# One layernorm pass for two nested ones, and query, key and value projections as three products of rounded float32 parts, in a Perceiver block on one core

## The chip, the cores and the metric

One core of a Trainium2 chip runs the whole program in one launch. The metric is the device time of that launch in microseconds (us), from runs of the same program; lower is better. Engines are named PE (TensorE, matrix products), ACT (ScalarE), DVE (VectorE), POOL (GpSimd) and SP (SyncE, which issues the DMAs).

## The reference, cut to what matters

A Perceiver block on 256 tokens of width 512: cross-attention to 4096 context rows, self-attention with 16 heads, and a feed-forward part (FFN) with quantised weights. What the change touches is the self-attention's entry:

```python
def _layernorm(x, axis=-1, eps=1e-05):
    m = jnp.mean(x, axis=axis, keepdims=True)
    v = jnp.var(x, axis=axis, keepdims=True)
    return (x - m) / jnp.sqrt(v + eps)
...
def _L0_attn_ref(X, ln_w, ln_b, W_in, W_out):
    mu = jnp.mean(X, axis=-1, keepdims=True)
    var = jnp.mean(jnp.square(X - mu), axis=-1, keepdims=True)
    Xn = (X - mu) * jax.lax.rsqrt(var + LN_EPS) * ln_w + ln_b
    qkv = jnp.einsum('bsd,df->bsf', Xn, W_in)
    Q, K, V = jnp.split(qkv, 3, axis=-1)
    ...
    return out + X
...
x = x + _L0_xattn_ref(_layernorm(x), ctx_512, ...)
x = x + _L0_attn_ref(_layernorm(x), ln_w, ln_b, W_in, W_out)
x = x + _L0_ffn_ref(_layernorm(x), w1, w2, w3)
```

So x is normalised to h1 (which is also added back as the residual), h1 is normalised again, scaled and shifted to Xn, and Xn goes through the projection to queries, keys and values. Everything is float32. In the FFN each weight matrix is divided by its mean magnitude, rounded and clipped to -1, 0 or 1.

## The kernel before, in words

Five instruction streams are written out by hand, one for each engine; semaphores alone tie them together, so the order within each stream is the order of the code. Tokens are handled as two tiles of 128. The cross-attention fills the first 450 us or so. It ends with the output products (L615 to L617): for each head and tile three products of rounded float32 parts (type f32r), high by high, high by low and low by high. ACT makes the high part of the output weights by a copy into f32r (L1002) and DVE the low part by a subtraction (L1212).

Then comes the stretch around the change.

DVE, for each tile t: the residual sum out of PSUM (L1346), a layernorm to h1 and a second one of h1 to z1. A layernorm is batch statistics (L1170), aggregation (L1174), an addition of epsilon (L1178), a wait for ACT's square root (L940), a reciprocal (L1182), one refining step on numbers of one column (L1185 to L1190), and the normalisation of 128x512 (L1194). Behind them DVE has, in this order: the rotation of the tile-0 key block (rotate, L1360 to L1366), the total of the magnitudes of w1 (weight_total, L1375), the rotation of the tile-0 query block, the copy of the tile-0 values (L1371), the mean and scale of w1 (L1380, L1383), the rotation of the key block of tile 1, the total of w3, the rotation of the query block, the scale of w3, the copies of the transposed keys (L1388), and then the softmax maxima (L1407), among which stand the clips of the rounded weights (L1427): w1 behind the fifth maximum, w3 behind the sixth.

PE: the transposes of z1 of tile 0 (L578) into bank 0, then `project(t, j)` (L767), four float32 products of 128x512 for tile t and j = 0, 1, 2 (key, query and value weights): (0,0), (0,1), the transposes of tile 1, (0,2), the weight sum of w1 (weight_sum, L758, which needs DVE's total), (1,0), (1,1), the weight sum of w3, the transposes of the rotated blocks with one half of (1,2) between them, the other half, and the attention scores (L809).

ACT: roots (L940); the scaling and shift of the transposed tile into hTn (scale_shift, L1054, four operations of 128x128 a tile); the absolute sums of w1, w3 and w2 (abs_sum, L1064), four for each; the copies of the projected blocks out of PSUM (natural_copy, L1070); the copies of the transposed queries (L1075). Its order is: roots, scale_shift(0), roots and two sums, natural_copy(0,0), two sums, natural_copy(0,1), scale_shift(1), three sums, natural_copy(1,0), two sums, natural_copy(1,1), and so on.

POOL: h1 is added to x_sb (L542), once for each tile, when the output products are done; then, as soon as DVE has the scale of w1 (L1383), w1 and w3 are scaled (L549) and rounded (L556) in eight pieces each; w2 follows when DVE has clipped w3.

SP: the loads of the projection weights wink_sb, winq_sb and winv_sb (L467 to L469) and of w1 (L470) when the last attention product is done, and those of w3, w2 and the output weights (L472 to L474) when the output products are done.

Of the kernel before, what the change touches and what calls it, by code (L numbers as in the profile page):

```python
# [6 lines left out]
TT = TOK // 128  # L7
DM = 512
DK = DM // 128
# [14 lines left out]
EPS = 1e-5  # L24
# [3 lines left out]
def program(nc, x_in, ctxT, kcos, ksin, qcos, qsin, wq, wkcq, wqr, wkr, wkv, wo,  # L28
# [24 lines left out]
    with ctx:  # L53
# [50 lines left out]
        v_sb = at("v_sb", C + 16 * KB, [128, TT, DM])  # L104
# [42 lines left out]
        acc = small("acc", [128, 2, 2, 128])  # L147
        cT = small("cT", [128, FG, TOK])
# [9 lines left out]
        eps = small("eps", [128, 1])  # L158
        rs = small("rs", [128, TT])
# [66 lines left out]
        hTn_done = sem("hTn_done")  # L226
        hTq_done = [sem(f"hTq_done{k}") for k in range(2)]
# [53 lines left out]
        win_in = sem("win_in")  # L281
# [88 lines left out]
        def _(sp):  # L370
# [96 lines left out]
            sp.dma_start(wink_sb[:, :, :], w_k).then_inc(win_in, 16)  # L467
            sp.dma_start(winq_sb[:, :, :], w_q).then_inc(win_in, 16)
            sp.dma_start(winv_sb[:, :, :], w_v).then_inc(win_in, 16)  # L469
# [12 lines left out]
        def _(pool):  # L482
# [57 lines left out]
            for t in range(TT):  # L540
                pool.wait_ge(z_done, TT + 2 * t + 1)
                nc.gpsimd.tensor_tensor(x_sb[:, t, :], x_sb[:, t, :], h1[:, t, :], ALU.add).then_inc(x2_done, 1)  # L542
# [32 lines left out]
        def _(pe):  # L575
# [184 lines left out]
            def project(t, j, chunks=range(DK)):  # L760

                w = (wink_sb, winq_sb, winv_sb)[j]
                pe.wait_ge(win_in, 48)
                for c in chunks:
                    if j == 0:
                        pe.wait_ge(hTn_done, t * DK + c + 1)
                    last = nc.tensor.matmul(bank(QKV_BANK[t][j]), hTn[:, c, t * 128:(t + 1) * 128], w[:, c, :],  # L767
                                            start=(c == 0), stop=(c == DK - 1))
                if c == DK - 1:
                    last.then_inc(qkv_done, 1)  # L770

            pe.wait_ge(z_done, TT + 2)
            tile_transposes(z1[:, 0, :], 0, zT_done)
            project(0, 0)
            pe.wait_ge(x1_done, TT)
            project(0, 1)
            pe.wait_ge(z_done, TT + 4)
            tile_transposes(z1[:, 1, :], 1, zT_done)
            project(0, 2)
            weight_sum(0, bank(7, 0, 1))  # L780
            project(1, 0)
            project(1, 1)
            pe.wait_ge(wmean_done, 1)
            weight_sum(1, bank(7, 0, 1))
            for t in range(TT):
                for j in range(2):
                    pe.wait_ge(rot_done, 2 * t + j + 1)
                    if t == 1 and j == 1:
                        pe.wait_ge(qT_done, 1)
                    tile_transposes(qkn[:, t, j, :], 2 if j == 1 else t, qkT_done)  # L790
                if t == 0:
                    pe.wait_ge(v_copied, 1)
                    project(1, 2, range(DK // 2))
            project(1, 2, range(DK // 2, DK))
# [142 lines left out]
        def _(act):  # L937
# [111 lines left out]
            def scale_shift(t):  # L1049
# [3 lines left out]
                for c in range(DK):  # L1053
                    nc.scalar.activation(hTn[:, c, t * 128:(t + 1) * 128], bank(t, c * 128, (c + 1) * 128), ACT.Identity,  # L1054
                                         bias=lnp[:, 1, c:c + 1], scale=lnp[:, 0, c:c + 1]).then_inc(hTn_done, 1)

# [21 lines left out]
            root(3, slice(0, 1))  # L1078
            root(4, slice(0, 1))
            scale_shift(0)  # L1080
            root(5, slice(1, 2))
            abs_sum(0, 0)
            root(6, slice(1, 2))
# [49 lines left out]
            root(7, slice(0, 1))  # L1133
# [3 lines left out]
            root(8, slice(1, 2))  # L1137
# [16 lines left out]
        def _(dve):  # L1154
# [185 lines left out]
            for h in range(len(SPLIT_STEPS), XH):  # L1340
                if h == 10:
                    context_low(XH // 2 - 1)
                output_weight_low(h)
            for t in range(TT):
# [3 lines left out]
                layernorm(x_sb, h1, t, t + 1)  # L1348
                dve.wait_ge(z_done, TT + 2 * t + 1)
                layernorm(h1, z1, t, t + 1)  # L1350
# [40 lines left out]
            rotate(0, 0)  # L1391
            weight_total(0)
# [64 lines left out]
            for t in range(TT):  # L1457
                dve.wait_ge(ao_done, t + 1)
                layernorm(x_sb, h2, t, t + 1, bank(6 + t), x3_done)
                dve.wait_ge(z_done, 3 * TT + t + 1)  # L1460
# [110 lines left out]
```

## Time and profile before

| what | value |
|---|---|
| median of 3 runs | 564.32 us (563.91 to 564.53) |
| span of the profiled execution | 564.2 us |
| busy: PE / DVE / ACT / POOL | 94% / 83% / 65% / 28% of the span |
| mean granted clock of PE | 0.991 of full |
| DMA | 107.41 MB, mean 190 GB/s |

The profiled execution is one run of its own; its time is its span, from the first to the last instruction, and it lies between the fastest and the median of the runs above. Times on the axis below are us from the start of the span. A "releaser" is what ended an engine's idle time. A float32 product of 128x512 shows as two records, a rounded one as one; products overlap, so a group's time is shorter than the sum of its records.

### The profile page before, as it was taken

Reading aid. Unit: us, or ns where it says so; the run is one execution under the profiler, and the core shown is the slowest. Engines: PE = TensorE matmul, PEld = TensorE weight load, DVE = VectorE, ACT = ScalarE, POOL = GpSimd, SP = SyncE. Lnnn points to the kernel's source line nnn. Section 1 sums busy time; section 2 is a strip of 40 time slices with the busy share of each in tenths; the row PEclk is TensorE's granted clock in tenths of the full one; section 3 lists DMA queues with packets and bytes.
Section 4 is the critical chain, followed back from the end, with each engine's and each line's share of the span. In section 5 each row is a group of like instructions: output and inputs, shape, how many; then the busy total and the mean of one; then the engine's idle time right before and its main releaser. Section 6 shows DMA issues by size and latency. Waiting matters only on the chain.

```text
span 564.2 us, 10021 instructions
## 1 busy us (share of the span) xinstructions
PE 528.2 (94%) x3799; PEld 353.0 (63%) x3803; DVE 468.4 (83%) x708; ACT 366.0 (65%) x447; POOL 159.0 (28%) x202
## 2 busy tenths in 40 slices
PE   7899976799999999999999999999997998999996
PEld 3767643366666666666667666766676784455443
DVE  3566997999989999999999999999996447478686
ACT  2125433888788688688688787787786444886441
POOL 2378965101202202202202202202000001496501
PEclk9989999999999999999999999999998998999999
DMA  8979468399999999999999999999999997500001
GB/s 314 345 259 288 156 116 220 87 200 196 198 195 200 202 197 203 208 209 212 203 204 195 203 204 194 198 210 195 204 198 178 226 416 305 238 1 1 1 0 38
DMA packets 287806, 107.41 MB, mean 190 GB/s; under 512 B 276896, under 2 KB 277920, under 8 KB 286368
## 3 DMA queue, kind: packets, MB, share of 16 engines
q1 hardware_dynamic: 287776, 107.01, 87.6%
q8 instruction: 18, 0.29, 0.2%
q14 instruction: 12, 0.10, 0.0%
HBM read 37.26 MB, written 0.52 MB: 67 GB/s over the span
## 4 chain that ended last, share of the span: by engine, by line
PE 57%; DVE 17%; POOL 8%; DMA 6%; issue 6%; ACT 4%; SPq 0%; ACTq 0%; DVEq 0%; POOLq 0%
PE ps L665 15%; PE ps L667 8%; PE ps L647 7%; PE ps L649 7%; PE ps L648 7%; DMA pT<-split 6%; POOL qrope L498 5%; DVE rows L1273 4%; DVE split L1255 3%; PE ps L767 3%; POOL keys L509 2%; POOL stage L510 1%; PE ps L876 1%; PE ps L615 1%; PE ps L617 1%
## 5 line engine op out<-in xcount | busy, mean ns | idle before, releaser
L665 PE MATMUL ps<-pT,VH 128*128 128x256 f16 x1024 | 196.6, 274 | 2.1 <-DMA pT<-split 2.0
L667 PE MATMUL ps<-pT,VL 128*128 128x128 f16 x1024 | 183.3, 220 | 0.0
L1273 DVE TENSOR_SCALAR_CACHE_REDUCE rows<-ps,qback 128x1024 f32<-128x1024 f32 x128 | 163.5, 1280 | 16.0 <-PE ps L649 15.9
L1033 ACT ACTIVATE split<-rows,rz 128x2048 f16<-128x2048 f32 x64 | 124.7, 1994 | 67.8 <-DVE rz L1221 67.7
L1255 DVE SCALAR_TENSOR_TENSOR split<-rows,rz,split 128x2048 f16<-128x2048 f32 x64 | 150.3, 2350 | 1.3 <-issue 1.2
L1019 ACT ACTIVATE rows<-rows,negm 128x2048 f32<-128x2048 f32 x64 | 127.2, 1987 | 0.2 <-DVE negm L1278 0.2
L665 PEld LDWEIGHTS ps<-pT,VH 128*128 128x128 f16 x1024 | 100.5, 98 | 42.6 <-DMA pT<-split 4.8
L667 PEld LDWEIGHTS ps<-pT,VL 128*128 128x128 f16 x1024 | 100.6, 98 | 27.5
L528 POOL TENSOR_TENSOR ctx_c<-acc 128x128 f32<-128x128 f32 x32 | 24.7, 772 | 296.8 <-ACT acc L1008 296.8
L647 PE MATMUL ps<-KH,qcur 128*128 128x512 f16 x256 | 97.1, 379 | 3.3 <-DVE rows L1273 3.3
L649 PE MATMUL ps<-KH,qcur 128*128 128x512 f16 x256 | 97.0, 379 | 0.0
L648 PE MATMUL ps<-KL,qcur 128*128 128x512 f16 x256 | 97.0, 379 | 0.0
L498 POOL TENSOR_TENSOR qrope<-qrope,qrot 128x384 f32<-128x384 f32 x32 | 38.2, 1214 | 22.6 <-DVE qrot L1311 22.4
L649 PEld LDWEIGHTS ps<-KH,qcur 128*128 128x128 f16 x256 | 25.0, 98 | 30.2
L696 PE MATMUL ps<-hTq,wq_sb 128*128 128x256 f32 x128 | 30.4, 392 | 1.5 <-ACT hTq L946 0.8
L647 PEld LDWEIGHTS ps<-KH,qcur 128*128 128x128 f16 x256 | 25.1, 98 | 10.2 <-DVE rows L1273 4.3
L1305 DVE TENSOR_TENSOR qrope<-ps,qcos_sb 128x768 f32<-128x768 f32 x16 | 15.2, 950 | 19.0 <-PE ps L707 18.9
L696 PEld LDWEIGHTS ps<-hTq,wq_sb 128*128 128x128 f32 x128 | 24.4, 195 | 7.5 <-issue 3.3
L648 PEld LDWEIGHTS ps<-KL,qcur 128*128 128x128 f16 x256 | 25.0, 98 | 2.3
L707 PE MATMUL ps<-qhk,wkcq_sb 128*128 128x256 f32 x96 | 23.7, 386 | 2.6 <-DVE qrot L1311 2.6
L549 POOL TENSOR_SCALAR w_sb<-w_sb,wscale 128x704 f32<-128x704 f32 x24 | 20.5, 872 | 14.1 <-DVE wscale L1383 9.9
L707 PEld LDWEIGHTS ps<-qhk,wkcq_sb 128*128 128x128 f32 x96 | 17.6, 190 | 7.1 <-issue 5.0
(175 smaller groups left out, 638.3 us busy)
## 6 DMA issues: line engine op xcount, KB each, us to landing
w_sb<-w SPq DMA_DIRECT2D x3, 2816.0 KB, 15.6
wq_sb<-wq SPq DMA_DIRECT2D x4, 1024.0 KB, 7.3
wo_sb<-wo SPq DMA_DIRECT2D x16, 256.0 KB, 4.2
wkcq_sb<-wkcq SPq DMA_DIRECT2D x4, 768.0 KB, 10.3
keys<-ctxT SPq DMA_DIRECT2D x8, 256.0 KB, 7.1
stage<-ctxT SPq DMA_DIRECT2D x16, 128.0 KB, 9.0
stage<-kcos SPq DMA_DIRECT2D x8, 256.0 KB, 9.0
stage<-ksin SPq DMA_DIRECT2D x8, 256.0 KB, 9.5
```

The lines of the kernel that those rows point to most:

```text
L498: nc.gpsimd.tensor_tensor(qrope[:, h % 4, part], qrope[:, h % 4, part], qrot[:, h % 2, part], ALU.add).then_inc(qrope_done, 1)
L647: nc.tensor.matmul(o, q[0], KH[:, key], start=True, stop=False)
L648: nc.tensor.matmul(o, q[0], KL[:, key], start=False, stop=False)
L649: last = nc.tensor.matmul(o, q[1], KH[:, key], start=False, stop=True)
L665: nc.tensor.matmul(bank(6 + r % 2, 0, 256), VH[:, 4 * b + k, :], p.rearrange("p x q -> p (x q)"), start=(b == 0 and k == 0), stop=False)
L667: last = nc.tensor.matmul(bank(6 + r % 2, 0, 128), VL[:, 4 * b + k, :], p[:, 0, :], start=False, stop=(b == 7 and k == 3))
L696: last = nc.tensor.matmul(bank(0, a * TOK, (a + 1) * TOK), wq_pair(wq_sb, q)[:, c, head], hTq[:, c, :], start=(c == 0), stop=(c == DK - 1))
L707: last = nc.tensor.matmul(ps[:, o:o + TOK], wkcq_sb[:, h // WQG % 2, h % WQG, c * 128:(c + 1) * 128], qhk[:, h, :], start=True, stop=True)
L1019: nc.scalar.activation(part, part, ACT.Exp, bias=negm[:, k:k + 1], accum_out=zpart[:, k, half:half + 1]).then_inc(exp_done, 1)
L1033: nc.scalar.activation(split[:, split_slot(r, half), :, 0, :], rows[:, k, half * 2048:(half + 1) * 2048].rearrange("p (b k) -> p b k", k=1 ...
L1255: nc.vector.scalar_tensor_tensor(out=split[:, split_slot(r, half), :, 1, :], in0=rows[:, k, half * 2048:(half + 1) * 2048].rearrange("p (b ...
L1273: nc.vector.tensor_scalar(rows[:, k, c * 1024:(c + 1) * 1024], ps[:, score_bank(s) * 512:(score_bank(s) + 2) * 512], qback[:, r // 2:r // ...
```

## The change

One pass of statistics serves both layernorms: DVE computes mean and variance v of x once and from them v + eps and v(1 + eps) + eps². ACT takes the roots of both in one operation, and DVE writes z1 (the twice normalised tile) first and h1 second, both directly from x. The second pass of statistics and its root are gone. POOL's residual add now waits for h1 by a semaphore of its own.

The projections use rounded float32 parts. ACT copies each of the three weight matrices into f32r (128x2048, one operation), DVE subtracts to get the low parts in place. ACT's scale_shift writes each tile twice: four operations into f32r (hTn_hi), then the four into hTn; DVE subtracts the one from the other (hTn_lo). PE then does high by high, high by low, and low by high, 12 products of 128x512 for each (t, j) in place of 4 float32 ones. Buffers move (v_sb, the new parts), and the three weight loads get a semaphore each.

```diff
-            sp.dma_start(wink_sb[:, :, :], w_k).then_inc(win_in, 16)
+            sp.dma_start(wink_sb[:, :, :], w_k).then_inc(win_in[0], 16)
...
             for t in range(TT):
-                pool.wait_ge(z_done, TT + 2 * t + 1)
+                pool.wait_ge(h1_done, t + 1)
...
+            def project_hi(t, j, chunks=range(DK)):
+                hi, lo = ((wink_hi, wink_lo), (winq_hi, winq_lo), (winv_hi, winv_lo))[j]
+                pe.wait_ge(win_hi_done, j + 1)
+                pe.wait_ge(win_lo_done, j + 1)
                 for c in chunks:
...
+                    pe.wait_ge(hTn_hi_done, t * DK + c + 1)
+                    for w in (hi, lo):
+                        nc.tensor.matmul(bank(QKV_BANK[t][j]), hTn_hi[:, t, c, :], w[:, c, :],
+                                         start=(c == 0 and w is hi), stop=False)
+            def project_lo(t, j):
+                pe.wait_ge(hTn_lo_done, t + 1)
+                for c in range(DK):
+                    last = nc.tensor.matmul(bank(QKV_BANK[t][j]), hTn_lo[t][:, c, :],
+                                            (wink_hi, winq_hi, winv_hi)[j][:, c, :], start=False, stop=(c == DK - 1))
+                last.then_inc(qkv_done, 1)
-            pe.wait_ge(z_done, TT + 2)
+            pe.wait_ge(z1_done, 1)
             tile_transposes(z1[:, 0, :], 0, zT_done)
-            project(0, 0)
+            project_hi(0, 0)
             pe.wait_ge(x1_done, TT)
-            project(0, 1)
-            pe.wait_ge(z_done, TT + 4)
+            project_hi(0, 1)
+            pe.wait_ge(z1_done, 2)
             tile_transposes(z1[:, 1, :], 1, zT_done)
-            project(0, 2)
+            project_lo(0, 0)
+            project_lo(0, 1)
+            project_hi(0, 2)
+            project_lo(0, 2)
             weight_sum(0, bank(7, 0, 1))
-            project(1, 0)
-            project(1, 1)
+            project_hi(1, 0)
+            project_lo(1, 0)
+            project_hi(1, 1)
+            project_lo(1, 1)
...
-                    project(1, 2, range(DK // 2))
-            project(1, 2, range(DK // 2, DK))
+                    project_hi(1, 2, range(DK // 2))
+            project_hi(1, 2, range(DK // 2, DK))
+            project_lo(1, 2)
...
                 for c in range(DK):
+                    nc.scalar.activation(hTn_hi[:, t, c, :], bank(t, c * 128, (c + 1) * 128), ACT.Identity,
+                                         bias=lnp[:, 1, c:c + 1], scale=lnp[:, 0, c:c + 1]).then_inc(hTn_hi_done, 1)
+                for c in range(DK):
...
+            def both_roots(t):
+                act.wait_ge(ve2_done, 2 * t + 2)
+                nc.scalar.activation(sd2[:, t, :], ve2[:, t, :], ACT.Sqrt).then_inc(sd_done, 1)
...
-            root(3, slice(0, 1))
-            root(4, slice(0, 1))
+            qkv_weight_high(0)
+            qkv_weight_high(1)
+            both_roots(0)
+            qkv_weight_high(2)
             scale_shift(0)
-            root(5, slice(1, 2))
+            both_roots(1)
             abs_sum(0, 0)
-            root(6, slice(1, 2))
             abs_sum(0, 1)
             natural_copy(0, 0)
...
+            qkv_weight_low(0)
+            qkv_weight_low(1)
             for t in range(TT):
                 dve.wait_ge(xo_done, t + 1)
                 nc.vector.tensor_tensor(x_sb[:, t, :], bank(2 + t), x_sb[:, t, :], ALU.add).then_inc(x1_done, 1)
                 dve.wait_ge(x1_done, t + 1)
-                layernorm(x_sb, h1, t, t + 1)
-                dve.wait_ge(z_done, TT + 2 * t + 1)
-                layernorm(h1, z1, t, t + 1)
+                two_layernorms(t)
+            normalised_low(0)
+            qkv_weight_low(2)
...
             rotate(0, 0)
+            normalised_low(1)
             weight_total(0)
             rotate(0, 1)
             value_copies(0)
```

The new functions of DVE, of which two_layernorms is statistics and aggregation as before, the two sums (ve2), the wait for the root, five operations on two columns, and the two normalisations:

```python
def qkv_weight_low(j):
    dve.wait_ge(win_hi_done, j + 1)
    nc.vector.tensor_tensor((wink_lo, winq_lo, winv_lo)[j][:, :, :].rearrange("p c d -> p (c d)"),
    ...
                            ALU.subtract).then_inc(win_lo_done, 1)
def normalised_low(t):
    dve.wait_ge(hTn_done, DK * (t + 1))
    nc.vector.tensor_tensor(hTn_lo[t][:, :, :], hTn[:, :, t * 128:(t + 1) * 128], hTn_hi[:, t].bitcast(f32),
                            ALU.subtract).then_inc(hTn_lo_done, 1)
def two_layernorms(t):
    ...
    nc.vector.tensor_scalar(z1[:, t, :], x_sb[:, t, :], mv[:, t, 0:1], rs2[:, t, 1:2],
                            ALU.subtract, ALU.mult).then_inc(z1_done, 1)
    nc.vector.tensor_scalar(h1[:, t, :], x_sb[:, t, :], mv[:, t, 0:1], rs2[:, t, 0:1],
                            ALU.subtract, ALU.mult).then_inc(h1_done, 1)
```

## Rows read from the trace of the kernel before

**Rows 1.** Page, part 1: busy us, share of the span, instructions.
```profile
PE 528.2 (94%) x3799; PEld 353.0 (63%) x3803; DVE 468.4 (83%) x708; ACT 366.0 (65%) x447; POOL 159.0 (28%) x202
```

**Rows 2.** Timeline of PE: start, us, line, tiles, count, idle before, releaser.
```profile
455.17 0.40 PE L616 MATMUL ps<-wo_lo,ctxl_hi 128*128 128x512 f32 x1
...
469.73 0.39 PE L617 MATMUL ps<-wo_hi,ctxl_lo 128*128 128x512 f32 x1
...
473.11 5.37 PE L767 MATMUL ps<-wink_sb,hTn 128*128 128x512 f32 x8 [0.64 <-ACT hTn L1054]
...
489.27 3.60 PE L767 MATMUL ps<-winq_sb,hTn 128*128 128x512 f32 x8
```

**Rows 3.** Timeline of DVE, the same columns.
```profile
464.71 0.69 DVE L1346 TENSOR_TENSOR x_sb<-ps,x_sb 128x512 f32<-128x512 f32 x1 [4.64 <-PE ps L617]
...
467.62 0.55 DVE L1194 TENSOR_SCALAR h<-x_sb,mv,rs 128x512 f32<-128x512 f32 x1
...
470.38 1.38 DVE L1194 TENSOR_SCALAR z<-h,mv,rs 128x512 f32<-128x512 f32 x1
...
486.61 0.16 DVE L1383 RECIPROCAL wscale<-wmean 128x1 f32<-128x1 f32 x1
...
511.97 2.46 DVE L1427 TENSOR_SCALAR w1b<-w1b 128x5632 bf16<-128x5632 bf16 x1
...
515.48 1.61 DVE L1427 TENSOR_SCALAR w3b<-w3b 128x5632 bf16<-128x5632 bf16 x1
```

**Rows 4.** Chain of waits, 425 to 565 us: start, us, engine, tile, line.
```profile
471.81 0.67 PE ps L578 x4
...
512.06 2.38 DVE w1b L1427
```

**Rows 5.** Stretches of 1 us: length, busy engines, PE clock, DMA, GB/s.
```profile
474.00:475.00 1.00, 1.00 (x2) 0.33 (x1) 0.61 (x4) 1.00 (x3) 0.00 (x0) 0.50 0.94 406
```

**Rows 6.** Timeline of ACT.
```profile
466.39 0.29 ACT L940 ACTIVATE sd<-mv,eps 128x1 f32<-128x1 f32 x1 [6.22 <-DVE mv L1174]
...
472.50 1.50 ACT L1054 ACTIVATE hTn<-ps,lnp 128x128 f32<-128x128 f32 x4 [3.06 <-PE ps L578]
...
478.51 0.60 ACT L1070 ACTIVATE qkn<-ps 128x512 f32<-128x512 f32 x1 [0.20 <-PE ps L767]
...
482.44 1.50 ACT L1054 ACTIVATE hTn<-ps,lnp 128x128 f32<-128x128 f32 x4
...
489.47 0.60 ACT L1070 ACTIVATE qkn<-ps 128x512 f32<-128x512 f32 x1 [1.18 <-PE ps L767]
...
492.91 0.60 ACT L1070 ACTIVATE qkn<-ps 128x512 f32<-128x512 f32 x1
```

**Rows 7.** Timeline of POOL.
```profile
475.75 1.26 POOL L542 TENSOR_TENSOR x_sb<-x_sb,h 128x512 f32<-128x512 f32 x1 [4.29 <-DVE h L1194]
486.87 7.17 POOL L549 TENSOR_SCALAR w_sb<-w_sb,wscale 128x704 f32<-128x704 f32 x8 [9.85 <-DVE wscale L1383]
...
506.98 5.97 POOL L556 TENSOR_SCALAR w3b<-w_sb 128x704 bf16<-128x704 f32 x8
```

**Rows 8.** By line and shape, 425 to 565 us: busy, mean ns, idle.
```profile
L1212 DVE TENSOR_TENSOR wo_lo<-wo_sb,wo_hi 128x512 fp32r<-128x512 f32 x16 | 10.3, 693 | 7.8 <-ACT wo_hi L1002 7.7
...
L1033 ACT ACTIVATE split<-rows,rz 128x2048 f16<-128x2048 f32 x2 | 4.0, 1995 | 0.1
```

**Rows 9.** Timeline of SP's DMA issues.
```profile
451.16 0.68 SPq L468 DMA_DIRECT2D winq_sb<-w_q  x1
```

**Rows 10.** DMA issues of 450 to 452.3 us: KB each, us to landing.
```profile
winq_sb<-w_q SPq DMA_DIRECT2D x1, 1024.0 KB, 9.3
```

**Rows 11.** What writes rot_tmp: count, duration ns least, median, most.
```profile
L1360 DVE TENSOR_TENSOR rot_tmp<-qkn,acs x4: 424/424/781, 479.1 to 493.5; 128x256 f32<-128x256 f32 x4
```

**Rows 12.** Timeline of PE, 106 to 118 us.
```profile
113.23 0.39 PE L647 MATMUL ps<-KH,qcur 128*128 128x512 f16 x1 [2.00 <-DVE rows L1273]
```

**Rows 13.** The same columns as rows 5, in a longer stretch.
```profile
80.00:120.00 40.00, 29.67 (x169) 14.50 (x168) 35.15 (x60) 24.62 (x36) 12.39 (x15) 1.00 0.76 165
```

## What the change should do to the time, worked out before it ran

> **What bounds the kernel now.** I read the page first: TensorE (PE) is busy 94% of the 564.2 us span [rows 1]. That is an average. The change touches only what follows the cross-attention, some 458 us on, so I read that stretch: first the chain of waits, then the timelines of PE, ScalarE (ACT), VectorE (DVE) and GpSimd (POOL), then the durations by line. The reader is to see four things.
>
> First, PE ends the output products at 470.12 (469.73 + 0.39 [rows 2]) and then stands, because z of the first tile is ready only at 471.76 (470.38 + 1.38 [rows 3]); the chain goes on with the transposes at 471.81 [rows 4]. Second, the six projections are full float32 and their PE time is the chain from there: the first takes 5.37 us, the fifth 3.60 [rows 2], because PE's granted clock was 0.50 in between, the lower of its two levels (1.2 of 2.4 GHz) [rows 5]. Third, ACT's queue holds, in one order, the copies that PE and DVE wait for and the absolute sums of the FFN weights; from the copy of the first query/key block at 478.51 to the last at 492.91 it stood still only 1.18 us [rows 6]. Fourth, the clip of w1 on DVE is on the chain [rows 4] and took 2.46 us, the equal clip of w3 1.61 [rows 3]: the first ran beside POOL's rounding of w3, which ended at 512.95 (506.98 + 5.97 [rows 7]); the clip ended 1.48 after that, nearly its whole length alone.
>
> **The change, part by part.** Times are on the axis of the profiled run; its span of 564.2 us stands 0.1 below the median of 564.32.
>
> *Splitting the weights.* Three rounded copies on ACT: 128x2048 takes 1.99 us [rows 8]. Three subtractions on DVE: 128x512 takes 0.69 [rows 8], so four times the length is at most 2.8, and about 2.2 if the fixed part is paid once. ACT and DVE are free from about 459 and 460; the query weights land at 460.5 (451.16 + 9.3 [rows 9, 10]). So the copies end at 461 and 463, the two subtractions ahead of the layernorm at 463.2 and 465.4. The first residual sum then starts about 0.7 after its 464.71 [rows 3]. I cost all this at nothing: PE's output products cover it until 470.12. Without that cover the 0.7 would count. The third copy and subtraction come later, below.
>
> *One set of statistics.* Before, the first layernorm of tile 0 ended at 468.17 (467.62 + 0.55 [rows 3]) and a second one followed. Now the normalised z comes at the end of the first, with about three small operations more (0.2 each): 468.17 + 0.6 + 0.7 = 469.4. That is before PE is free, so the transposes start at 470.1, 1.7 us earlier. What is late next is the ACT copy out of PSUM.
>
> *ACT writes each tile twice.* Eight scalings in place of four, which took 1.50 [rows 6]: 470.6 to 473.4. PE starts on the first chunk at about 471.2 and needs 16 rounded products for the first two high parts. 64 intervals between 455.17 and 469.73 [rows 2] give 0.2275 us each, so 3.6 us, to 474.8. The root for tile 1 is queued behind the eight scalings: 473.4. From root to end of the normalisation took 1.78 (466.39 [rows 6] to 468.17), now 1.9: z of tile 1 at 475.2, its transposes at 475.9.
>
> *The low part of tile 0.* PE next wants the low products, and these wait for a DVE subtraction (128x512, 0.69 alone) queued behind both outputs of tile 1: it starts at 475.8, just when POOL starts its residual add, 1.26 us long [rows 7]. Beside POOL, z took 1.38 where the same operation takes 0.55 alone [rows 3], and an operation with two SBUF inputs 0.78 for 0.42 [rows 11]. Bounds: not slowed, done at 476.5; held off wholly, 477.7. I take 477.1, by the two-input row, the nearest. The Trainium skill, "GPSIMD Engine Reference", section Key points, says that POOL shares its SBUF interfaces with VectorE and contends with instructions that have two SBUF inputs; by it the 476.5 drops out. It does not say which side waits; the rows do, DVE. Four low products (0.9) follow, so ACT's first copy comes at 478.2 against 478.51: all the earlier start is back to 0.3.
>
> *ACT's line from there.* 14.40 us before (478.51 to 492.91), less 1.18 idle, plus four more scalings of tile 1 (1.4): 14.6. The last copy stands at 492.8 against 492.91.
>
> *A new wait on PE.* The weight sum sits in PE's order between the tiles and needs a total from DVE. DVE's total is now queued behind the low part of tile 1, which needs ACT's eighth scaling of tile 1. Before, those scalings began 3.93 after the first copy (482.44 [rows 6]); now they begin at 482.1, eight last 2.9, so 485.0. Subtraction to 485.7, total to 485.9. PE, done with tile 0 at 482.2, stands about 3.8 us. Then the key projection of tile 1 takes 12 x 0.2275 = 2.7, to 488.8; ACT comes to its copy at 489.4, so this wait is hidden if the clock stays up.
>
> *The projections themselves.* Three rounded products take 0.68 against 0.86 for a float32 one (3.60 for four, overlaps left out [rows 2]), so PE does some 4.3 us less work in all. It is off the path: ACT and DVE set the pace now. On the path is the second half of the last projection, 8 x 0.2275 = 1.82 against 1.72: +0.1. So the scores start within 0.1 of before; call this shift d = 0, with bounds -0.7 (low part not slowed) and +1.2 (clock, below).
>
> *POOL.* Its 26.1 us of weight rounding (486.87 to 512.95 [rows 7]) starts on the weight scale, which DVE computed at 486.61 [rows 3]. Now DVE has, after the total at 485.9, a rotation (four operations, 1.3 by the 0.42 [rows 11]), a value copy (0.7) and two small ones: 488.2. POOL starts 1.6 later and ends at 514.5. The clip of w1 waits at its old place, 512.0 + d, and if POOL holds it off as before it ends at 514.5 + 1.48 = 516.0 against 514.43. The DVE operations behind it are on the chain, so **+1.55 us** reaches the end. A d below 1.5 is swallowed by it. SP issues the same loads in the same order, with one semaphore each in place of a common one, which I cost at nothing.
>
> Sum: 564.2 + 1.5, plus 0.1 to the median: 565.7 us.
>
> **The rivals.**
>
> *A, the clip is not held longer than before.* If DVE gets in between POOL's instructions, only d is left: 564.3 to 565.4. For: there were only two POOL instructions left beside the clip before. Against: it finished 1.48 after POOL, so it had got almost nothing done beside it.
>
> *B, the low part of tile 0 is held off wholly, or PE's clock falls before it.* Then ACT's line and POOL's start move 0.6 to 1.0 further, and the end with them: 566.3 to 567.2. For the hold: z beside the same POOL add. PE would stand about 0.6 and 1.2 us around the transposes; before, stands of 1.7 and 0.64 [rows 2] were followed by the lower clock [rows 5], but one of 2.00 was not [rows 12, 13].
>
> *C, the clock falls in the 3.8 us stand.* A fall after less standing is in the trace [rows 2, 5], so I hold it likely. The price is bounded by the first projection of before, 5.37 against 3.60: up to 1.7 us on PE, 0.5 of it hidden, so d = 1.2: under the 1.55, no change of the forecast; with A, 565.4. The Trainium skill, "TensorE: Matmul & The Clock Gate", Part 1, says the throttled state is the default and activity releases it; by it the fall is all but certain.
>
> *D, faster.* The subtraction of tile 0 is not slowed by POOL (done by 476.5) and the clip is not held: ACT's line is 0.7 earlier, rotations of tile 1 have more of POOL's late start free of contention (up to 0.8, half of the 1.6 by which it is later), and the clip may run at its 1.61 (-0.85), so 562.0 to 563.6. The point that decides is whether the first query/key copy comes before 477.6. Against: both rows of contention.
>
> *E, the change does not do what it says:* no sign; the weights are split on the chip and three products stand in the code.
>
> **How the numbers follow.** Forecast 0.51 (565.2 to 566.2, by 0.5 either way on POOL's end, which is also the likeliest case's own range), A with or without C 0.20, B 0.13, D 0.16. The forecast's point is 565.7. Leaving out the lower three quarters of D and the top of B gives 563.2 to 567.0. A measurement tells this kernel from no change at about 0.2%, 1.13 us: faster means below 563.2, slower above 565.45. Faster: three quarters of D, 0.12. Slower: three quarters of the forecast's band lie above 565.45, 0.38, with nearly all of B: 0.5. The rest, 0.38, is the same.
>
> **What would show it.** Transposes at about 470.1; first copy on ACT at 478.2; PE standing some 3.8 us ahead of the weight sum, released by DVE's total at 485.9; POOL starting at 488.4 and ending at 514.5; the clip of w1 at 3.5 us or more. Wrong would be: a first copy before 477.6, a last one after 494, a POOL start before 487.5, or a clip that ends before POOL does.

## The result, and the profile after

| | before | after |
|---|---|---|
| median of 22 runs of each, same chips | 564.64 us (560.98 to 566.95) | 566.93 us (565.39 to 572.37) |
| ratio of the runs, 95% interval | | 1.0046 (1.0029 to 1.0064) |
| profiled execution: span, mean granted clock of PE | 564.2 us, 0.991 | 570.5 us, 0.982 |
| end of the output products, on its own axis | 470.12 us | 475.25 us |
| **tail**: from there to the end of the span | 94.08 us | 95.25 us |

The change costs half a per cent: +2.3 us between the medians, where +1.4 was forecast.

Two things have to be settled before the two profiles are compared. First, a run's time is about 1.8 us more than its span (after: 572.37 against 570.5; the runs below give 1.75 to 1.91). So the profiled run of before, with its span of 564.2, took about 566.0 us: it stands above all three runs of the table ahead of the prediction, and not between them as is said there. The profiled run of after is the slowest of its 22. Second, the spans differ by 6.3 us, but 5.1 of that has built up by the end of the output products, which come 5.13 us later. In that run PE's granted clock was low in two stretches more than in before's, 11 to 15 and 96 to 100 us, and this row is from the first of them (stretches of PE: length, busy us, PE clock, DMA share, GB/s):

```profile
13.00:14.00 1.00, 1.00 (x4) 0.50 1.02 395
```

The runs don't put this down to the change: e1 and e2, which split the weights just as after does, have one such stretch each and end the output products at 468.97 and 469.94 us, the four profiles without the change have one to three and end them at 469.22 to 472.35, and after has four. So everything below is read on another axis: "+x" is x us after the end of the last output product, in each kernel's own profile.

The busy shares of the page say nothing of it; PE's is 93% for 94% [rows 1]:

```profile
PE 530.0 (93%) x3823; PEld 360.2 (63%) x3827; DVE 473.8 (83%) x703; ACT 373.7 (65%) x456; POOL 162.2 (28%) x202
```

PE's timeline after (columns as in [rows 2]) shows where the time goes:

```profile
474.86 0.39 PE L636 MATMUL ps<-wo_hi,ctxl_lo 128*128 128x512 f32 x1
475.10 0.60 PE L597 MATMUL ps<-ident,z 128*128 128x128 f32 x4
476.33 0.47 PE L787 MATMUL ps<-wink_hi,hTn_hi 128*128 128x512 f32 x1 [0.64 <-ACT hTn_hi L1086]
...
481.41 1.19 PE L794 MATMUL ps<-wink_hi,hTn_lo 128*128 128x512 f32 x4 [0.40 <-DVE hTn_lo L1403]
...
490.22 0.58 PE L777 MATMUL ps<-wtot,ones 128*128 128x1 f32 x2 [3.56 <-DVE wtot L1461]
490.66 0.78 PE L787 MATMUL ps<-wink_hi,hTn_hi 128*128 128x512 f32 x1
...
494.22 1.88 PE L794 MATMUL ps<-wink_hi,hTn_lo 128*128 128x512 f32 x4
...
497.78 1.07 PE L794 MATMUL ps<-winq_hi,hTn_lo 128*128 128x512 f32 x4
```

The transposes follow the products without the 1.69 us that PE stood before. Then PE stands 3.56 us for DVE's total, a wait that before did not have (its weight sum followed the products with no idle time), and behind it the key projection of tile 1 runs from 490.66 to 496.10: 5.4 us, where twelve products at the spacing of [rows 2] take 2.7. Its last four take 1.88, those of the query projection right behind 1.07. The stretches give the reason (length, busy us of PE, PE's weight loads, DVE, ACT and POOL, PE clock, DMA share, GB/s):

```profile
491.00:492.00 1.00, 1.00 (x3) 0.80 (x3) 1.00 (x3) 1.00 (x1) 0.00 (x0) 0.50 1.04 442
...
494.00:495.00 1.00, 1.00 (x3) 0.79 (x3) 0.00 (x0) 0.00 (x0) 1.00 (x2) 0.50 0.00 0
```

PE's clock is at its lower level (1.2 of 2.4 GHz), and in the second of these stretches DVE and ACT stand idle: they wait for this projection. DVE's timeline (columns as in [rows 3]):

```profile
480.67 0.69 DVE L1403 TENSOR_TENSOR hTn_lo<-hTn,hTn_hi 128x512 fp32r<-128x512 f32 x1
...
484.33 1.41 DVE L1452 TENSOR_TENSOR qkn<-rot_tmp 128x256 f32<-128x256 f32 x1
489.40 0.69 DVE L1403 TENSOR_TENSOR hTn_lo<-hTn,hTn_hi 128x512 fp32r<-128x512 f32 x1 [3.66 <-ACT hTn L1089]
490.01 0.15 DVE L1461 TENSOR_REDUCE wtot<-wpart 128x1 f32<-128x4 f32 x1
...
492.06 0.16 DVE L1469 RECIPROCAL wscale<-wmean 128x1 f32<-128x1 f32 x1
...
518.99 1.62 DVE L1514 TENSOR_SCALAR w1b<-w1b 128x5632 bf16<-128x5632 bf16 x1
```

ACT's, as in [rows 6]:

```profile
482.64 0.60 ACT L1117 ACTIVATE qkn<-ps 128x512 f32<-128x512 f32 x1 [1.05 <-PE ps L794]
...
496.14 0.60 ACT L1117 ACTIVATE qkn<-ps 128x512 f32<-128x512 f32 x1 [2.41 <-PE ps L794]
...
499.56 0.58 ACT L1117 ACTIVATE qkn<-ps 128x512 f32<-128x512 f32 x1
```

and POOL's, as in [rows 7]:

```profile
475.34 1.27 POOL L561 TENSOR_TENSOR x_sb<-x_sb,h 128x512 f32<-128x512 f32 x1 [18.39 <-PE ps L636]
480.83 4.62 POOL L561 TENSOR_TENSOR x_sb<-x_sb,h 128x512 f32<-128x512 f32 x1 [4.22 <-DVE h L1425]
492.32 6.97 POOL L568 TENSOR_SCALAR w_sb<-w_sb,wscale 128x704 f32<-128x704 f32 x8 [6.87 <-DVE wscale L1469]
...
512.39 5.97 POOL L575 TENSOR_SCALAR w3b<-w_sb 128x704 bf16<-128x704 f32 x8
```

The low part of tile 0 (480.67) is not slowed beside POOL's residual add; the add is, 4.62 us for its usual 1.26 [rows 7], and behind it the last operation of DVE's rotation (484.33) takes 1.41 us, where its like at 490.93 takes 0.42. And the clip of w1 (518.99) begins 0.63 us after POOL's rounding ended (512.39 + 5.97 = 518.36) and takes 1.62, not 2.46 as in [rows 3]. The chain of waits that ended last is now this (columns as in [rows 4]):

```profile
487.98 1.40 ACT hTn L1089 x4
489.44 0.57 issue
490.22 0.58 PE ps L777 x2
490.80 3.62 PE ps L787 x8
494.42 1.69 PE ps L794 x4
496.14 0.60 ACT qkn L1117
...
521.91 1.53 DVE w3b L1514
```

The clip of w1 has left it, the low part of tile 1 and the slow projection have come in.

### The profile page after: what moved, and what is told of

Same layout as the page of the kernel before. It is cut to its first block, busy times and chain, and to the rows that moved or that the text cites. A ratio compares the mean times of both kernels' runs of the same rounds, so it can differ in the third digit from the quotient of the medians.

```text
span 570.5 us, 10076 instructions
## 1 busy us (share of the span) xinstructions
PE 530.0 (93%) x3823; PEld 360.2 (63%) x3827; DVE 473.8 (83%) x703; ACT 373.7 (65%) x456; POOL 162.2 (28%) x202
## 4 chain that ended last, share of the span: by engine, by line
PE 57%; DVE 16%; POOL 8%; issue 7%; DMA 6%; ACT 5%; SPq 0%; ACTq 0%; DVEq 0%; POOLq 0%
PE ps L684 15%; PE ps L686 8%; PE ps L666 7%; PE ps L668 7%; PE ps L667 7%; DMA pT<-split 6%; POOL qrope L517 5%; DVE rows L1321 4%; DVE split L1303 3%; POOL keys L528 2%; PE ps L634 1%; PE ps L636 1%; POOL stage L529 1%; PE ps L635 1%; PE ps L908 1%
## 5 line engine op out<-in xcount | busy, mean ns | idle before, releaser
L715 PE MATMUL ps<-hTq,wq_sb 128*128 128x256 f32 x128 | 31.7, 404 | 1.5 <-ACT hTq L978 0.8
L737 PE MATMUL ps<-qrope,wqr_sb 128*64 128x256 f32 x96 | 13.4, 418 | 8.8 <-POOL qrope L517 7.8
```

Of the source, the lines that this page charges most:

```text
L715: last = nc.tensor.matmul(bank(0, a * TOK, (a + 1) * TOK), wq_pair(wq_sb, q)[:, c, head], hTq[:, c, :], start=(c == 0), stop=(c == DK - 1))
```

## The experiments

All tails, measured as above. The clip column gives start and length of the clip of w1; "low clock" the us after the products in which PE's granted clock was under 1, the last 2 us of a span left out ("end only": nowhere else). Each row is one profiled run. Tail and median time don't agree to better than a us or two: e9 and e10 are below before in the median (0.997 and 0.9976) with tails of 92.39 and 93.30 against e11's 92.48.

| kernel | tail | first / last copy on ACT | POOL start / end of w3 rounding | scores | clip of w1 | low clock |
|---|---|---|---|---|---|---|
| before | 94.08 | 8.39 / 22.79 | 16.75 / 42.83 | 29.02 | 41.85, 2.46 | 3 to 7 |
| e11, before | 92.48 | 8.10 / 21.09 | 15.05 / 41.20 | 27.34 | 40.18, 2.50 | none |
| e12, before | 92.43 | 8.09 / 21.09 | 15.05 / 41.13 | 27.32 | 40.16, 2.45 | none |
| after | 95.25 | 7.39 / 24.31 | 17.07 / 43.11 | 30.90 | 43.74, 1.62 | 13 to 20 |
| e1 order | 92.53 | 7.39 / 21.79 | 13.61 / 40.19 | 28.13 | 40.96, 1.62 | 22 to 25 |
| e2 warm | 95.66 | 7.38 / 21.80 | 17.07 / 43.28 | 27.30 | 40.14, 4.62 | 49 to 56 |
| e3 one layernorm | 90.57 | 4.93 / 19.18 | 13.14 / 39.28 | 25.42 | 38.27, 2.49 | none |
| e4 parts only | 100.18 | 12.07 / 26.49 | 21.77 / 47.97 | 32.00 | 44.85, 4.60 | 11 to 15, 52 to 59 |
| e5 before, warm | 92.35 | 8.09 / 21.09 | 15.05 / 41.12 | 27.32 | 40.15, 2.46 | end only |
| e6 late add | 95.64 | 7.38 / 24.18 | 17.06 / 44.35 | 30.16 | 42.99, 2.83 | 13 to 20 |
| e7 warm, late clips | 97.01 | 7.39 / 21.80 | 17.08 / 43.29 | 27.32 | 46.27, 1.62 | 70 to 77 |
| e8 split on DVE | 95.23 | 7.16 / 19.54 | 12.62 / 39.21 | 25.53 | 44.46, 1.62 | 67 to 74 |
| e9 one layernorm, clips | 92.39 | 4.93 / 19.19 | 13.15 / 39.28 | 25.42 | 41.10, 1.62 | 49 to 52 |
| e10 split on DVE, clips | 93.30 | 7.20 / 19.57 | 12.63 / 39.12 | 26.18 | 41.85, 1.62 | 50 to 54 |

**e1: the low part of tile 1 behind the weight scale.** PE's weight sum of w1 then waits for no subtraction.

```diff
             rotate(0, 0)
-            normalised_low(1)
             weight_total(0)
...
             weight_scale(0, bank(7, 0, 1))
+            normalised_low(1)
```

> Times count from the end of the output products; the tail is from there to the end of the span (94.1 us in the profile before, 95.3 in the one after). Theory 1, PE's stand on the total of w1 and the half clock behind it are the loss: with the low part of tile 1 moved behind the scale of w1 on VectorE, the stand shrinks below 1.3 us, the last query/key copy comes at +22.0 (after: +24.3), the scores at +28.3 (after: +30.9), GpSimd's rounding starts at +13.5 (after: +17.1), and the tail is 92.7, the time 564.3. Rival, ScalarE's extra scalings and the splitting are the loss and the stand is covered: the stand only moves in front of the low products of tile 1, the scores stay at +30.9, the tail at 95.3, the time at 566.9.

Measured: 563.38 us, 0.9984 (0.9952 to 1.0016) of before. PE no longer stands for the total of w1, only 1.15 us for the low part, in the middle of the key projection and without a fall of the clock there. It does stand 2.61 us for the total of w3 later, and there the clock falls (22 to 25 in the table):

```profile
480.21 0.28 PE L777 MATMUL ps<-wtot,ones 128*128 128x1 f32 x2
480.79 0.47 PE L787 MATMUL ps<-wink_hi,hTn_hi 128*128 128x512 f32 x1 [0.30 <-ACT hTn_hi L1086]
...
484.03 1.19 PE L794 MATMUL ps<-wink_hi,hTn_lo 128*128 128x512 f32 x4 [1.15 <-DVE hTn_lo L1403]
...
490.58 0.35 PE L777 MATMUL ps<-wtot,ones 128*128 128x1 f32 x2 [2.61 <-DVE wtot L1461]
```

One moved operation takes the whole loss away: the interval lies below that of after (1.0029 to 1.0064), and the tail is 2.7 us shorter than after's and equal to e11's. The order on DVE is the cause of the loss against before. The move does two things at once, the scores come 2.8 us earlier than in after (28.13) and POOL starts 3.5 us earlier (13.61), and the clip, which starts behind POOL's rounding here too, is not held. e2 does only the first of the two.

**e2: the stand filled.** PE multiplies an identity matrix into a bank that is overwritten, while it waits for the total.

```diff
             project_lo(0, 2)
+            keep_busy(15, 7)
             weight_sum(0, bank(7, 0, 1))
```

> 15 empty products in front of the weight sum fill PE's stand, nothing else is changed. Theory 1, the lower clock behind the stand cost 2.4 us of the projection: it takes 2.7 us in place of 5.1, the last copy comes at +21.9, the scores at +28.4. Then the clip of w1 starts at +41.4, before GpSimd ends its rounding at +43.1: if it is held as in the kernel before, it takes about 3.2 us and the tail is 94.5 (time 566.1); if it is not held it takes 1.6, tail 92.8 (time 564.4). Rival, the clock is no part of it: scores at +30.9, tail 95.3, time 566.9 or more by the fill.

Measured: 567.92 us, 1.0051 (1.002 to 1.0083). The clock stays up and the scores start 3.6 us earlier than after (27.30 against 30.90), yet the tail is 0.4 us longer. DVE's and POOL's timelines show what takes the place of the slow projection:

```profile
510.08 4.62 DVE L1515 TENSOR_SCALAR w1b<-w1b 128x5632 bf16<-128x5632 bf16 x1
```

```profile
507.23 5.99 POOL L575 TENSOR_SCALAR w3b<-w_sb 128x704 bf16<-128x704 f32 x8
```

The clip now meets POOL's rounding and ends at 514.70, 1.48 after the rounding ends at 513.22. The clip is 2.12 us longer than e11's 2.50, and longer than the 3.2 that was expected. Another 1.1 comes behind it on PE:

```profile
518.06 1.12 PE L854 MATMUL ps<-ident,prob 128*128 128x128 f32 x8 [2.24 <-ACT pT L1165]
519.11 1.97 PE L842 MATMUL ps<-kT,qT 32*128 32x256 f32 x8
```

DVE's next maximum is queued behind the held clip, so PE stands 2.24 us, its clock falls, and eight score products take 1.97 in place of 1.13. From the end of the clip to the end of the span it is 50.90 us here and 49.8 to 50.0 in before, e11, after, e1 and e3. e4 has the same: clip of 4.60, a stand of 2.23 us, low clock, 50.73.

**e3: the single layernorm alone,** with the projections in float32 as before (four products, `project` as it was, no parts of weights or of hTn).

```diff
-            project_hi(0, 0)
+            project(0, 0)
...
-            project_lo(0, 0)
-            project_lo(0, 1)
-            project_hi(0, 2)
-            project_lo(0, 2)
+            project(0, 2)
```

> The single pass of statistics alone, projections in float32 as before. Theory 1: the transposes start 1.7 us earlier, PE does not fall to half clock in the first projection (1.8), the first copy comes at +5.1, the last at +19.3, the scores 3.5 us earlier than before, tail 90.6; against the median of before, where not every run has that fall, 561.5. Rival, the layernorm's gain is given back on ScalarE's line as in the kernel after: first copy at +8, tail 94, time 564.6.

Measured: 561.22 us, 0.994 (0.9911 to 0.9969). The first copy on ACT comes 3.17 us earlier than in e11, all else 1.9 earlier, and the clip, held just as before (2.49), ends 1.9 earlier. e1, which differs from it by the parts alone, has a tail 2.0 us longer.

**e4: the parts alone,** with the two layernorms of before.

```diff
-                two_layernorms(t)
+                layernorm(x_sb, h1, t, t + 1)
+                dve.wait_ge(z_done, TT + 2 * t + 1)
+                layernorm(h1, z1, t, t + 1)
```

> The rounded parts alone, with the two layernorms of before. Theory 1: the first transposes come 2.4 us later than in the kernel after and everything behind them with them, tail 97.6, time 569.2. Rival, ScalarE's line or PE's stand hides the layernorm: tail 95.3, time 566.9.

Measured: 571.61 us, 1.0115 (1.0064 to 1.0167), more than either expectation. The tail is 7.7 us longer than e11's. In the order on PE the low products of tile 0 stand behind the transposes of tile 1, and these wait for its second layernorm:

```profile
479.24 0.66 PE L597 MATMUL ps<-ident,z 128*128 128x128 f32 x4 [2.91 <-DVE z L1244]
479.84 1.32 PE L794 MATMUL ps<-wink_hi,hTn_lo 128*128 128x512 f32 x4
```

So the first copy comes at 12.07, and later the clip is held as in e2. Together with the single layernorm the parts cost 2.8 against e11 and not 7.7; the layernorm alone gains 1.9 (e3). The two halves do not add.

**e5: before, with PE kept busy in its stand of 1.69 us** before the transposes.

```diff
+            keep_busy(8, 1)
             pe.wait_ge(z_done, TT + 2)
```

> The kernel before, with 8 empty products in PE's stand ahead of the first transposes. Theory, the half clock in its first projection belongs to some runs and not to the kernel: with the fill the first projection takes 3.6 us in place of 5.4, the last copy comes at +21.0 (before: +22.8), the tail is 92.3 in place of 94.1; the median falls by 1.8 times the share of runs that have the fall, about 0.9, to 563.7. Rival, the fall moves to another place or is no loss: tail 94.1, time 564.6.

Measured: tail 92.35, as expected, but 565.64 us, 1.0006 (0.9982 to 1.003), not lower. If the fall of the clock in [rows 5] were in every run of before, filling the stand would give 1.7 us, a ratio of 0.997; that lies outside, unless the fill itself costs something. A fall in half of the runs would be inside. e11 and e12 point the same way: the fall is in one of three profiles of before.

**e6: POOL's residual add of tile 1 behind the rounding of w1.**

```diff
+            residual_add(0)
...
             weight_round(0, w1_sb, w1b)
+            residual_add(1)
```

> The kernel after, with GpSimd's residual add of tile 1 moved behind the rounding of w1, so that VectorE's subtractions and the first rotation run with GpSimd idle. Theory, VectorE's operations with two inputs are served and GpSimd's add waited (4.62 us for 1.27): the low part of tile 0 stays at 0.69 us, the first copy at +7.4, the last operation of the first rotation takes 0.42 in place of 1.41, the tail stays at 95.3. The prediction's step, GpSimd slows the subtraction: the first copy comes earlier than +7.4.

Measured, a single run: 569.45 us, tail 95.64. The add takes 1.27 there, and the last operation of the first rotation 0.43 in place of 1.41. The first copy, POOL's start and the weight sum do not move (7.38, 17.06, and PE stands 3.60), so the contention around the add is real and delays none of them. The tail says less: the scores come 0.74 us earlier than in after, but the moved add stands in POOL's row of weight work, whose rounding of w3 ends 1.24 us later and holds the clip (2.83).

**e7: e2 with both clips later,** behind the seventh and eighth maximum, clear of POOL.

```diff
-                if v in (2, 3):
-                    clip(v - 2, (w1b, w3b)[v - 2])
+                if v in (4, 5):
+                    clip(v - 4, (w1b, w3b)[v - 4])
```

> The kernel with PE's stand filled, and the clips of w1 and w3 two places later in VectorE's order, behind the seventh and eighth maximum, where GpSimd has ended the rounding of w3. Theory, the clip held by GpSimd's rounding gave back what the clock gained: both clips take 1.6 us, scores at +27.3, tail 92.7 in place of 95.7, time 565.0 in place of 567.9. Rival, the hold is not on the path or the later clips delay the rounding of w2 onto it: tail 95.7, time 567.9.

Measured: 569.41 us, 1.0086 (1.0055 to 1.0117). The clips take 1.62 each, but POOL's scaling and rounding of w2 start only when w3 is clipped, and now DVE waits for that; the tail is longer than both expectations:

```profile
531.16 1.63 DVE L1515 TENSOR_SCALAR w2b<-w2b 128x5632 bf16<-128x5632 bf16 x1 [4.84 <-POOL w2b L575]
```

**e8: hTn by DVE in place of ACT,** out of PSUM, with the order of e1, a third sum on ACT ahead of its first copy, and the late clips of e7.

```diff
-                    nc.scalar.activation(hTn[:, c, t * 128:(t + 1) * 128], bank(t, c * 128, (c + 1) * 128), ACT.Identity,
-                                         bias=lnp[:, 1, c:c + 1], scale=lnp[:, 0, c:c + 1]).then_inc(hTn_done, 1)
...
+                    nc.vector.tensor_scalar(hTn[:, c, t * 128:(t + 1) * 128], bank(t, c * 128, (c + 1) * 128),
+                                            lnp[:, 0, c:c + 1], lnp[:, 1, c:c + 1], ALU.mult, ALU.add).then_inc(hTn_done, 1)
```

> The kernel after, with what the runs so far point to: VectorE and not ScalarE writes the second, float32 copy of each normalised tile, behind ScalarE's rounded one; the low part of tile 1 behind the scale of w1; a third sum of w1 ahead of the first copy on ScalarE; the two clips behind the seventh and eighth maximum. Theory, ScalarE's line and the order on VectorE set the pace: first copy at +6.6, last at +19, scores at +25, GpSimd starts at +11.5, the clips take 1.6, tail 89.5, time 560.5. Rival, PE or VectorE is the bound at +22 all the same: tail 92, time 563.

Measured: 567.2 us, 1.0034 (1.0006 to 1.0062). The scores start at 25.53, the earliest of all kernels with parts, and it is lost again at the same place as in e7 (DVE waits 4.81 us for the rounded w2): tail 95.23, where theory and rival had 89.5 and 92.

**e9 and e10: both clips behind the sixth maximum,** in e3 and in e8.

```diff
-                if v in (2, 3):
-                    clip(v - 2, (w1b, w3b)[v - 2])
+                if v == 3:
+                    clip(0, w1b)
+                    clip(1, w3b)
```

> The single pass of statistics alone (float32 projections), and both clips behind the sixth maximum on VectorE, where GpSimd has just ended its rounding. Theory, the 0.85 us by which GpSimd held the clip of w1 in the run with one layernorm pass come back: both clips take 1.6, tail 89.7 in place of 90.6, time 560.4. Rival, the two clips in a row delay a later maximum by as much: tail 90.6, time 561.2.

> The split on VectorE with both clips behind the sixth maximum, so that the rounding of w2 starts some 5 us earlier than in the run before. Theory, that rounding was the bound there (VectorE waited 4.8 us for it): scores at +25.5, tail 90.0, time 561. Rival, another wait on VectorE stands behind it: tail 92 or more, time 563.

Measured: e9 563.6 us, 0.997 (0.995 to 0.999), tail 92.39; e10 563.85 us, 0.9976 (0.9955 to 0.9998), tail 93.30. The rival of e10 came true; e9's tail lies above both that were expected. Neither clip is held, and still e9's tail is 1.8 us longer than e3's. PE's timeline of e9 shows the price:

```profile
516.56 1.94 PE L840 MATMUL ps<-ident,prob 128*128 128x128 f32 x8 [2.24 <-ACT pT L1145]
518.43 0.64 PE L860 MATMUL ps<-pT,v_sb 128*32 128x256 f32 x2
```

Two clips in a row are 3.1 us in which DVE gives out no maximum; behind them PE stands the same 2.24 us as in e2, and its clock falls; e10 has the same stand and the same fall. Where two places were tried in one kernel, the old one was the better (e3 against e9, e2 against e7), and both behind the sixth maximum better than the late one (e10 against e8).

**e11 and e12: before, unchanged.**

> The kernel before, unchanged, as a kernel of its own, to see how much of its spread lies in the stretch of the change. Theory: ratio 1.000; each run's time lies 1.8 above its span; the tail is 92.35 where PE keeps its clock in the first projection and 94.1 where it doesn't, and most runs are of the first kind, so that the profiled run of before, with 94.1, stood above the median. Rival, the fall is in nearly every run: tail 94.1.

> One more look at the kernel before, unchanged. Theory: a tail of 92.35 or of 94.1 and no other; the rest of the spread lies ahead of the end of the output products. Rival: tails in between or outside, so that the stretch of the change has other causes of spread.

Measured: 564.91 us, 1.0 (0.9974 to 1.0026), and 565.75 in the one run of e12. The tails are 92.48 and 92.43; e11's first projection takes 3.67 us, where [rows 2] had 5.37:

```profile
472.21 3.67 PE L767 MATMUL ps<-wink_sb,hTn 128*128 128x512 f32 x8 [0.64 <-ACT hTn L1054]
```

**The version that beats both is e3**: one layernorm pass, float32 projections, 0.6% under before.

## Why the prediction was right or wrong

The sign and the range held (566.93, just inside 567.0); the size did not, and neither did the mechanism. +1.4 us was forecast, +2.3 measured. Two steps failed. The baseline took a slow first projection, 1.6 us of it, as the kernel's own, though two of three profiles of before lack it. And the sum put +1.55 us on a clip held by POOL and let it swallow a d (the shift of the scores) of at most 1.2; in after the clip is not held, and d is 1.9 us against the profiled run of before (30.90 for 29.02) and 3.6 against e11, because PE's clock fell in the stand and the key projection took 5.4 us for 2.7. On the tail the sum came out nearly (+1.17 measured against +1.55), and that is luck: d, less the 0.84 by which the clip is shorter, happened to stand where the held clip was put. (The sum as written, 564.2 + 1.5 + 0.1, gives 565.8 and not 565.7; nothing hangs on it.)

*Right: the place and the first half.* The transposes follow the products at once (forecast 470.1, measured 0.15 before the products' end). The weight split costs little: the first residual sum came 0.4 us later against the products (forecast 0.7). The stand before the weight sum was forecast at 3.8 us with the total at 485.9, that is +15.8; it was 3.56 us and +14.76. ACT's line from the first copy to the last was forecast at 14.6 us; with the clock kept up (e2) it is 14.42.

*Wrong: the baseline.* The step "its span of 564.2 us stands 0.1 below the median" compared a span with times that are 1.8 us longer than spans. The run behind the rows stood 1.4 above the median of the 22, and 1.6 to 1.7 of its tail was the slow first projection [rows 2, 5], which e11 and e12 do not have. I took a row that occurs in some runs as the kernel's own. Against the profiled run the tail grew by 1.17 us, against e11 and e12 by 2.8; the interval of the timed runs, 1.6 to 3.6 us, holds the second and not the first.

*Wrong: the price of the clock* (rival C: "up to 1.7 us on PE, 0.5 of it hidden, so d = 1.2: under the 1.55, no change of the forecast"). The fall came as held likely, but it took 2.7 us on PE (5.4 for 2.7), little of it was hidden (ACT's copy waited 2.41, and the last copy comes 2.5 later than in e2), and it pushed the last rotation on DVE from beside POOL's scaling of w1 to beside its rounding, where it took 3.5 us, against 2.4 in e2. Together d was 3.6 (30.90 against 27.30). The bound came from a float32 projection that ran only partly at the lower level; a stand twice as long was followed by a longer stretch at it.

*Wrong: which side waits.* The step "It does not say which side waits; the rows do, DVE" read z and the rotations [rows 3, 11] as the rule. Of the subtraction and the add, POOL's add waited: 4.62 us for 1.26, beside DVE operations at their length alone (0.69 and 2.28). So the first copy came at +7.39, not +8.1, and POOL's work started at +17.07, not +18.3. e6, where no add stands beside the subtraction, has the same two times: the subtraction lost nothing. The Trainium skill, "GPSIMD Engine Reference", Key points, names the contention; the runs show that it falls on either engine. The rows show what goes with it, the order of start: where DVE waited, POOL's add had begun 0.18 us ahead of z (470.20 against the 470.38 of [rows 3]; e5, e11 and e12 have the same), and where POOL waited, DVE's subtraction had begun 0.16 ahead of the add (480.67 and 480.83). The prediction put both starts at 475.8, so that by these rows the side was open.

```profile
470.20 1.27 POOL L542 TENSOR_TENSOR x_sb<-x_sb,h 128x512 f32<-128x512 f32 x1 [18.39 <-PE ps L617]
```

*The held clip: the mechanism is in other kernels, not in after.* I added 1.55 us for it and let it swallow d. In after, d is so large that the clip starts behind POOL and is not held at all: d of 3.56 against e11, less 0.88 for the shorter clip, is 2.68 of the 2.77 us by which the tail is longer. In e2, without the fall, the clip is held for 4.62 us as forecast (3.5 or more) and ends 1.48 behind POOL; it costs 2.12 and what comes behind it 1.10, less 0.04 by which it starts earlier: the 3.18 us by which that tail is longer than e11's. The two prices replace one another: with the fall alone removed (e2) the hold is paid, and e1, which also starts POOL earlier, pays neither. That e2's tail lies 1.58 above the profiled run's, as the forecast did, is chance: POOL ended 1.1 us earlier than forecast (43.28 against 44.4), and the second stand was not in the sum.

*The rivals.* A came true in its words only: the clip is not held, but since it starts behind POOL's end and not because DVE gets in between, and with a time that A did not allow, since its d ended at 1.2. B's 566.3 to 567.2 has the measured 566.93 in it by chance: the low part was not held, and the clock did not fall before it (it is full up to +13). D's condition, the first copy before 477.6, came true as well (470.12 + 7.39 = 477.51), and the kernel was not faster: what decided lay behind it, in the stand. Of the four signs of being wrong, three came: that first copy, a last copy after 494 (+24.31, or 494.43) and a POOL start before 487.5 (+17.07, or 487.19). What I didn't weigh is the two halves of the change apart, −1.9 us for the layernorm (e3 against e11) and +4.7 for the parts on top of it (95.25 against 90.57).

What stays open is in how many runs of after the fall behind the 3.56 us stand occurs. It is in both profiles that have the stand unfilled (after, e6), and since e2, which has no such stand, is no faster in the median, the end does not depend on it much.

## What to carry to other kernels

Before a profiled run is used as the axis of a sum, bring it to the runs' own unit, and look in a second profile for any stall that hangs on PE's clock; one that is not in both is a risk and not a row. When a reduction or a total that PE needs is queued behind new work on another engine, the price is the stand plus the slow work behind it, and moving one operation (e1) may be all that is needed. Where a long vector operation stands beside POOL work of fixed length, an earlier start on the critical path can be taken back by it, as in e2, so shift POOL's start and the path together.

## What the runs showed of the hardware that was not expected

- POOL's two-input add of 128x512 took 4.61 to 4.63 us in six profiles (after, e1, e2, e7, e8, e10), while DVE ran two-input subtractions of 0.69 and 2.28 us at their full pace beside it; it took 1.26 to 1.30 in all others. In all six the first subtraction began 0.16 or 0.17 us ahead of the add, and the second ran at full pace although the add had begun by then; the add ended at 485.45 in after, ahead of the rotation's slowed last operation. Beside the add of tile 0, which began 0.18 us ahead of it, DVE's z, with one SBUF tensor as input, took 1.38 for 0.55 [rows 3].
- A clip on DVE that begins under POOL's rounding ends 1.47 to 1.49 us after it in all eight profiles that have this (before, e2 to e6, e11, e12), however early it began: 2.45 to 4.62 us for 1.62. It gets almost nothing done beside POOL. The Trainium skill, "Advanced Engine Details and Errata", VectorE Performance Modes, says that VectorE instructions in a two-port mode and GpSimd's block each other; that the clip is one no run shows, and by these rows it is the clip that waits.
- PE's granted clock fell behind stands of 2.23 or 2.24 us in e2, e4, e9 and e10, not behind one of 1.61 at the same place in e11 or e3, and behind 1.69 plus 0.64 us in one profile of before out of three. The Trainium skill, "TensorE: Matmul & The Clock Gate", Part 1, says that the number of products at the lower clock differs from run to run of one kernel; the three profiles of before bear it out (5.37 us in one, 3.67 in the two others, for the same eight records).
